# Selections of two sets of heads issued in turn into two PSUM banks, and the places they take in the order of work

## The chip, the cores and the metric

The kernel runs on one core of one Trainium2 chip. The metric is device time in microseconds (us), the median of several runs of the whole program. Engines are named as in the profile: PE (TensorE matmul), PEld (its weight loads), DVE (VectorE), ACT (ScalarE), POOL (GpSimd), SP (SyncE, here only the issuer of DMAs; SPq is its queue).

## The reference

A decoder layer for 32 sequences of 128 tokens with 128 channels, all in float32: causal self-attention with 16 heads of 8 channels, one-head cross-attention to a context, and a mixture of 8 experts (top 2) with a shared expert. Cut to what matters here:

```python
def attn(x, W_attn, b_attn, W_proj, b_proj):          # x (32, 128, 128)
    q, k, v = split(x @ W_attn.T + b_attn)            # 16 heads of 8 channels
    f = cos(ang) + sin(ang)                           # (T, 8)
    att = einsum('bhqd,bhkd->bhqk', q * f, k * f) / sqrt(8)
    att = softmax(where(causal, att, min))
    y = einsum('bhqk,bhkd->bhqd', att, v)
    return y @ W_proj.T + b_proj
x = x + attn(layernorm(x), ...)
x = x + cross_attn(ctx, ctx, layernorm(x), ...)
x = x + moe(layernorm(x), ...)       # probs = softmax(x @ router_w.T), top 2 of 8
```

## The kernel before, in words

The attention stage is a software pipeline over the 32 batches b (sequences). Time is cut into slots s = -4, -3, ...; each entry of the list ORDER is (stage, ahead, part, which), and in slot s every engine goes through the list from top to bottom and does its own share of stage `name` for batch b = s + ahead, if `which` is None or b % 4 == which. So the one list is the program order of PE, ACT, DVE, POOL and SP at once, and each engine is strictly in order. Engines wait for one another by semaphores only.

Batches are projected in groups of four. Two kinds of slot hold selections. A **P slot** (s % 4 == 2) projects the next group (turn_x, project, halves) and selects its first two batches (`("select", 2, j, 0)`). An **R slot** (s % 4 == 3) selects the other two (`("select", 3, j, 2)`), and from slot 11 on it also holds `route`, the choice of experts for an earlier group. P slots are -2, 2, ..., 26; R slots are -1, 3, ..., 27. The steady pattern of four slots repeats; slot s begins at the scores of batch s with part 0.

**select(b, j)**: q and k of a group lie transposed in `qk_hi` and `qk_lo` (a high and a low part), 128 rows by 512 tokens; rows 32j to 32j+31 are the four heads of set j. A selection picks these 32 rows, for two batches, into 96 rows of a PSUM bank: four matmuls (k = 0, 1 for q and k; hi and lo accumulated), 32 rows in, 96 out, 256 columns each. The sets j = 0, 1, 2, 3 use different row groups of the PE array and the four shared banks 1, 3, 2, 0 (`BANK["select"]`). ACT then copies the bank to `qk_stack` (L898), 96 x 512. SP's stack_lo(b) copies from `qk_stack` to `k_slots` and `q_slots` by DMA, once all four sets are there.

**The shared banks.** Every use of one of the four banks is a numbered fill, in the order of the list (`bank_fills`). `w.bank_free(item)` makes PE wait until the reader of the bank's last content has signalled (`drained`); `w.bank_filled(item)` makes the reader wait for PE. Who lies in which bank around the selections:

- bank 0: turn_x2, select 3, values, tall_sums. `values` (PE, L678, 32 records) is probabilities times v.
- bank 1: turn_y, turn_ffn, router, project_v, select 0.
- bank 2: attn_out, xproject, turn_x, project, ranks, select 2.
- bank 3: turn_max, xscores, turn_xprobs, xout, select 1. `xscores` is read by ACT's Exp (L945) after DVE's maximum (L1172); `xout` is read by DVE (L1182).

**Other work near the selections.** `scores(b, j)`: PE L652 and L653 into ps_scores, read by DVE's row maximum L1128. `scores_t(b, j)`: PE L668, read by ACT's Exp L911, then masked on POOL (L551). `route(g)`: DVE L1209 to L1234 in a row; ACT's part is one Exp (L964), for which DVE waits ahead of L1229. `rstd_xattn` is ACT L926 and L928. `attn_out` is PE L697, for which PE waits until ACT has copied the transposed y (L922). `tall_sums` (PE L686, read by DVE L1134) and `turn_y` (PE L692, which waits for DVE's yn, L1137) end a batch's self-attention. `turn_ffn` is PE L734.

In a P slot the places of the selections were, among others: ..., scores 3, scores_t 0, **select 3**, xout, **select 2**, **select 0**, scores_t 1, tall_sums, **select 1**. In an R slot: ..., xscores, scatter, attn_out, **select 0**, norm_ffn, **select 3**, **select 1**, route, rstd_xattn, scores 2, project_v, norm_xattn, **select 2**, values, ... (norm_ffn has no PE work).

After the stage follow the scatter of rows to the experts, the experts' tiles, the shared expert and the output; each hangs on the end of the stage before it.

## Time and profile before

| | |
|---|---|
| median of 3 runs | 520.73 us (518.72 to 522.56) |
| the profiled execution's own time | 523.42 us |
| its span, first to last instruction | 521.7 us |
| mean granted PE clock over the span | 0.945 of full speed |
| granted PE clock between 60 and 300 us | 1.00 |
| instructions | 12081 |

Busy time is the union of an engine's instructions. Matmuls are pipelined, so the records of PE overlap, and what one matmul adds to the chain is less than its own duration. Where the profile gives an idle time of an engine, the engine and line behind the arrow are those that ended it. "issue" is idle time that nothing in the profile explains.

### The profile page before, as it was taken

Reading aid. Unit: us, or ns where it says so; the run is one execution under the profiler, and the core shown is the slowest. Engines: PE = TensorE matmul, PEld = TensorE weight load, DVE = VectorE, ACT = ScalarE, POOL = GpSimd, SP = SyncE. Lnnn points to the kernel's source line nnn. Section 1 sums busy time; section 2 is a strip of 40 time slices with the busy share of each in tenths; the row PEclk is TensorE's granted clock in tenths of the full one; section 3 lists DMA queues with packets and bytes.
Section 4 is the critical chain, followed back from the end, with each engine's and each line's share of the span. In section 5 each row is a group of like instructions: output and inputs, shape, how many; then the busy total and the mean of one; then the engine's idle time right before and its main releaser. Section 6 shows DMA issues by size and latency. Waiting matters only on the chain.

```text
span 521.7 us, 12081 instructions
## 1 busy us (share of the span) xinstructions
PE 447.5 (86%) x3494; PEld 348.2 (67%) x3494; DVE 387.7 (74%) x1262; ACT 320.9 (62%) x975; POOL 282.5 (54%) x369
## 2 busy tenths in 40 slices
PE   1566999999999999999899978459799999898993
PEld 1344667777677677677677756348588877787783
DVE  4473677788988988979889886878467766566585
ACT  1133778888778779788887867542355544454530
POOL 6604263362584775756755666446156655555581
PEclk9967999999999999999999999568899999999997
DMA  6612222221222222222222312512133322222194
GB/s 184 159 38 55 53 57 59 52 64 48 68 70 65 73 72 58 77 66 65 77 59 72 83 41 92 156 37 85 47 83 90 84 81 82 71 76 81 53 355 122
DMA packets 66998, 43.13 MB, mean 83 GB/s; under 512 B 9211, under 2 KB 63878, under 8 KB 66934
## 3 DMA queue, kind: packets, MB, share of 16 engines
q1 hardware_dynamic: 61876, 33.04, 23.6%
q0 software_dynamic: 4320, 8.99, 5.3%
q8 instruction: 30, 0.49, 0.4%
q10 hardware_dynamic: 738, 0.33, 0.2%
q14 instruction: 34, 0.28, 0.2%
HBM read 17.39 MB, written 12.09 MB: 57 GB/s over the span
## 4 chain that ended last, share of the span: by engine, by line
PE 43%; DVE 24%; DMA 11%; issue 8%; SPq 5%; ACT 4%; POOL 3%; DVEq 0%; ACTq 0%; POOLq 0%
PE ps_scores L809 6%; DMA ys<-ctx_t,late 5%; DVE negmax L1128 5%; DMA late<-xs 4%; PE ps_shared L634 3%; PE ps_shared L826 3%; PE ps_shared L678 3%; PE ps_scores L652 3%; PE ps_scores_t L668 3%; PE ps_scores L653 3%; PE ps_shared L622 3%; SPq L415 2%; DMA k_slots<-qk_stack 2%; PE ps_shared L817 2%; PE ps_shared L686 2%
## 5 line engine op out<-in xcount | busy, mean ns | idle before, releaser
L551 POOL TENSOR_SCALAR_AFFINE_SELECT probs<-probs 128x512 f32<-128x512 f32 x128 | 79.9, 635 | 93.6 <-ACT probs L911 92.4
L1128 DVE TENSOR_REDUCE negmax<-ps_scores 128x4 f32<-128x512 f32 x128 | 86.4, 683 | 24.7 <-PE ps_scores L653 24.4
L574 POOL DMA_INDIRECT ys<-ctx_t,late x71 | 68.4, 963 | 61.2 <-ACT ctx_t L1009 58.7
L911 ACT ACTIVATE probs<-ps_scores_t 128x512 f32<-128x512 f32 x128 | 74.4, 596 | 10.4 <-PE ps_scores_t L668 9.5
L544 POOL DMA_INDIRECT xs<-xrow,posu x64 | 65.1, 1017 | 24.8 <-DVE rsum L1250 13.5
L653 PE MATMUL ps_scores<-k_slots,qk_stack 96*128 96x512 f32 x128 | 78.0, 612 | 0.0
L809 PE MATMUL ps_scores<-wide,qk_stack 128*128 x213 | 69.5, 436 | 0.0
L668 PE MATMUL ps_scores_t<-wide,qk_stack 97*128 97x512 f32 x128 | 58.6, 464 | 1.1 <-issue 1.1
L652 PE MATMUL ps_scores<-causal,ident 128*128 128x512 bf16 x128 | 51.1, 399 | 7.8 <-DMA k_slots<-qk_stack 7.6
L1334 DVE COPY probs<-ps_shared 128x256 f32<-128x256 f32 x71 | 30.2, 425 | 25.3 <-PE ps_shared L817 25.3
L999 ACT ACTIVATE qk_stack<-ps_scores_t 128x128 fp32r<-128x128 f32 x71 | 19.7, 278 | 45.9 <-PE ps_scores_t L801 45.9
L826 PE MATMUL ps_shared<-wd,probs 128*128 x284 | 44.2, 279 | 0.1
L1004 ACT ACTIVATE vst<-ps_scores 128x256 f32<-128x256 f32 x71 | 27.3, 384 | 21.3 <-PE ps_scores L809 21.3
L898 ACT ACTIVATE qk_stack<-ps_shared 96x512 fp32r<-96x512 f32 x64 | 35.1, 591 | 8.0 <-PE ps_shared L634 7.5
L809 PEld LDWEIGHTS ps_scores<-wide,qk_stack 128*128 128x128 f32 x213 | 36.2, 195 | 3.2 <-issue 0.2
L826 PEld LDWEIGHTS ps_shared<-wd,probs 128*128 128x128 f32 x284 | 37.8, 193 | 0.4 <-issue 0.3
L678 PE MATMUL ps_shared<-probs,vst 128*32 128x128 f32 x1024 | 35.4, 280 | 0.2 <-POOL probs L551 0.2
L1328 DVE SCALAR_TENSOR_TENSOR vst<-vst,late,ps_scores 128x256 f32<-128x256 f32 x71 | 33.5, 472 | 1.2 <-ACT vst L1004 1.2
L1323 DVE TENSOR_TENSOR qk_stack<-ps_scores_t,qk_stack 128x128 fp32r<-128x128 f32 x71 | 20.7, 292 | 17.1 <-ACT qk_stack L999 13.8
L678 PEld LDWEIGHTS ps_shared<-probs,vst 128*32 128x32 f32 x1024 | 26.6, 111 | 8.2 <-issue 6.9
L668 PEld LDWEIGHTS ps_scores_t<-wide,qk_stack 97*128 97x128 f32 x128 | 25.2, 197 | 8.5 <-issue 3.3
L634 PE MATMUL ps_shared<-qk_hi,picks 32*96 32x256 f32 x128 | 26.8, 322 | 4.2 <-DVE qk_lo L1116 2.4
(229 smaller groups left out, 1163.9 us busy)
## 6 DMA issues: line engine op xcount, KB each, us to landing
k_slots<-qk_stack SPq DMA_DIRECT2D x128, 48.0 KB
wide<-qk_stack SPq DMA_DIRECT2D x128, 48.0 KB
late<-xs SPq DMA_DIRECT2D x71, 66.0 KB
wide<-ys SPq DMA_DIRECT2D x8, 512.0 KB, 7.4
ctx_t<-in_ctx SPq DMA_DIRECT2D x32, 64.0 KB, 2.0
out_x<-res SPq DMA_DIRECT2D x8, 256.0 KB, 3.4
ys<-ctx_t,late POOLq DMA_INDIRECT x71, 2.2
wd<-in_L_ffn_w_down SPq DMA_DIRECT2D x8, 128.0 KB, 3.5
```

The source lines that it names most:

```text
L544: pool.indirect_dma_start(out=xs, out_offset=bass.IndirectOffsetOnAxis(ap=posu[:, g % 2, k, u:u + 1], axis=0), in_=xrow[:, g % 2, k, u, :] ...
L551: pool.affine_select(out=part, in_=part, compare_op=ALU.is_ge, fill=0.0, base=0, pattern=[[0, HJ], [1, T]], channel_multiplier=-1).then_in ...
L574: pool.indirect_dma_start(out=ys, out_offset=bass.IndirectOffsetOnAxis(ap=xload_i[:, i % XL, C + 1:C + 2], axis=0), in_=ybuf[:, i % 4, :], ...
L634: mm = pe.matmul(part, picks[r, k, n].rearrange("p i a d -> p (i a d)"), m[r, k, cs], start=(n == 0), stop=(n == 1))
L652: pe.matmul(PS[j % 2][:], ident16[:], causal[:].rearrange("p a t -> p (a t)"), start=True, stop=False)
L653: pe.matmul(PS[j % 2][:], qk_stack[0:KR, b % RING, j, :], k_slots[:, b % 2, j].rearrange("p a t -> p (a t)"), start=False, stop=True)\
L668: pe.matmul(PT[j % 2][:], qk_stack[0:KR + 1, b % RING, NJ + j, :], q_slots[:, b % 4, j].rearrange("p a t -> p (a t)"), start=True, stop=Tr ...
L678: mm = pe.matmul(bank[VW * i:VW * (i + 1), j * T:(j + 1) * T], vst[:, b % 4, h, :], probs[:, b % 2, h, :], start=True, stop=True, skip_gro ...
L809: mm = pe.matmul(PS[i % 2][:], a[:, i % 4, :], m[:, bass.ds(e, 1), :].rearrange("p a f -> p (a f)"), start=(r == 0), stop=(r == 2))
L826: mm = pe.matmul(PM[i % 2][:, 0:C], xhT[:, i % 3, f * 128:(f + 1) * 128], wd[:, bass.ds(e, 1), f, :].rearrange("p a c -> p (a c)"), start= ...
L911: act.activation(probs[:, b % 2, j * HJ:(j + 1) * HJ, :].rearrange("p a t -> p (a t)"), PT[j % 2][:], ACT.Exp)\
L1128: dve.reduce_max(negmax[:, b % 2, j * HJ:(j + 1) * HJ], PS[j % 2][:].rearrange("p (i t) -> p i t", i=HJ), axis=AX.X, negate=True).then_inc ...
```

## The change

The selections of two sets of heads form a pair. At the place of set 0 in the list PE now issues set 0 and set 1, at the place of set 3 set 3 and set 2: it waits for both banks, and then issues the four matmuls of each in turn, one of the one, one of the other. At the places of sets 1 and 2 PE does nothing. The list is changed so that sets 1 and 2 stand right behind their partners; this moves ACT's copies as well, and the numbering of the bank fills. Nothing is computed otherwise.

```diff
 ORDER = [ ...
     ("halves", 2, 0, 0),
     ("norm_x_stats", 4, None, 0),
     ("select", 3, 0, 2),
+    ("select", 3, 1, 2),
     ("project_v", 1, None, 1),
     ("norm_ffn", -6, None, None),
     ("select", 3, 3, 2),
+    ("select", 3, 2, 2),
     ("norm_x", 3, None, 0),
-    ("select", 3, 1, 2),
     ("route", -11, None, 0),
     ("rstd_xattn", -3, None, None),
     ("scores", 0, 2, None),
...
     ("project_v", 1, None, 0),
-    ("select", 3, 2, 2),
     ("values", -2, None, None),
...
     ("select", 2, 3, 0),          # unchanged
     ("xout", -5, None, None),
     ("select", 2, 2, 0),
     ("select", 2, 0, 0),
+    ("select", 2, 1, 0),
     ("scores_t", -1, 1, None),
     ("tall_sums", -2, None, None),
     ("ranks", -11, None, 0),
-    ("select", 2, 1, 0),
 ]

             def select(b, j):
-                bank = w.bank_free(("select", b, j))
+                if j in (1, 2):
+                    return
+                pair = (j, (1, 0, 0, 2)[j])
+                banks = [w.bank_free(("select", b, i)) for i in pair]
                 w.ge(qk_split, 2 * (b // GB + 1))
-                if b == 0 and j == 0:
+                if b == 0:
                     pe.wait_ge(picked, 1)
-                r, cs = slice(32 * j, 32 * (j + 1)), slice(b % GB * T, (b % GB + 2) * T)
+                cs = slice(b % GB * T, (b % GB + 2) * T)
                 for k in range(2):
-                    part = bank[0:KR, k * 2 * T:(k + 1) * 2 * T]
                     for n, m in enumerate((qk_hi, qk_lo)):
-                        mm = pe.matmul(part, picks[r, k, n]..., m[r, k, cs], start=(n == 0), stop=(n == 1))
-                mm.then_inc(put_bank(("select", b, j)), 1)
+                        for i, bank in zip(pair, banks):
+                            r = slice(32 * i, 32 * (i + 1))
+                            mm = pe.matmul(bank[0:KR, k * 2 * T:(k + 1) * 2 * T], picks[r, k, n]..., m[r, k, cs],
+                                           start=(n == 0), stop=(n == 1))
+                            if k == 1 and n == 1:
+                                mm.then_inc(put_bank(("select", b, i)), 1)
```

## Rows read from the trace of the kernel before

**Rows 1.** From the page's first part: engine, busy us (share of the span), instructions.

```profile
PE 447.5 (86%) x3494; PEld 348.2 (67%) x3494; DVE 387.7 (74%) x1262; ACT 320.9 (62%) x975; POOL 282.5 (54%) x369
```

**Rows 2.** Window, four steady slots: us, busy of PE, PEld, DVE, ACT, POOL; clock; DMA.

```profile
161.30:197.32 36.02, 34.20 (x319) 25.59 (x319) 31.67 (x116) 29.74 (x92) 23.32 (x32) 1.00 0.26 69
```

**Rows 3.** Chain of waits, 182 to 206 us: start us, us, what.

```profile
193.73 0.64 PE ps_shared L634 x4
...
194.78 0.65 PE ps_shared L634 x8
...
196.30 0.64 PE ps_shared L634 x4
...
198.85 0.48 DVE negmax L1128
```

**Rows 4.** Windows within an R slot.

```profile
195.45:200.28 4.83, 4.83 (x32) 3.46 (x32) 3.12 (x9) 4.79 (x14) 2.44 (x4) 1.00 0.13 33
198.90:215.20 16.30, 15.41 (x152) 11.43 (x150) 15.43 (x70) 13.54 (x43) 9.65 (x15) 1.00 0.26 70
```

**Rows 5.** Timeline of PE: start us, us, what [idle before <-releaser].

```profile
215.48 0.30 PE L692 MATMUL ps_shared<-ident,yn 128*128 128x128 f32 x1 [0.56 <-DVE yn L1137]
```

**Rows 6.** Timeline of a P slot.

```profile
194.71 0.37 PE L634 MATMUL ps_shared<-qk_hi,picks 32*96 32x256 f32 x2
...
195.07 0.34 DVE L1182 SCALAR_TENSOR_TENSOR res<-ps_shared,xinv,late 128x128 f32<-128x128 f32 x1
...
195.45 1.08 ACT L898 ACTIVATE qk_stack<-ps_shared 96x512 fp32r<-96x512 f32 x2 [0.45 <-PE ps_shared L634]
...
196.42 0.59 ACT L911 ACTIVATE probs<-ps_scores_t 128x512 f32<-128x512 f32 x1
...
196.98 0.59 ACT L898 ACTIVATE qk_stack<-ps_shared 96x512 fp32r<-96x512 f32 x1
```

**Rows 7.** Timeline of the start-up.

```profile
26.66 0.51 PE L634 MATMUL ps_shared<-qk_hi,picks 32*96 32x256 f32 x4 [2.39 <-DVE qk_lo L1116]
...
27.36 2.05 ACT L898 ACTIVATE qk_stack<-ps_shared 96x512 fp32r<-96x512 f32 x4 [1.65 <-PE ps_shared L634]
```

**Rows 8.** Timeline of an R slot with a route.

```profile
198.78 0.27 ACT L922 ACTIVATE ynT<-ps_shared 128x128 f32<-128x128 f32 x1
...
199.20 0.46 PE L697 MATMUL ps_shared<-wpT,ynT 128*128 128x128 f32 x2
...
200.09 0.19 ACT L945 ACTIVATION_READ_ACCUMULATOR xprobs<-ps_shared,xneg 128x1 f32 x1
200.32 1.56 ACT L898 ACTIVATE qk_stack<-ps_shared 96x512 fp32r<-96x512 f32 x3
200.33 0.15 PEld L634 LDWEIGHTS ps_shared<-qk_hi,picks 32*96 32x96 f32 x1 [0.26 <-ACT xprobs L945]
...
200.87 0.55 DVE L1213 TENSOR_TENSOR sel<-iota,ix 128x32 f32<-128x32 f32 x2
...
201.77 0.23 ACT L964 ACTIVATE mx<-mx 128x36 f32<-128x36 f32 x1
...
202.76 0.16 DVE L1229 TENSOR_SCALAR cwg<-mx 128x4 f32<-128x4 f32 x1
```

**Rows 9.** Timelines of ACT, then DVE, in the first R slot with a route.

```profile
128.29 1.56 ACT L898 ACTIVATE qk_stack<-ps_shared 96x512 fp32r<-96x512 f32 x3
129.74 0.23 ACT L964 ACTIVATE mx<-mx 128x36 f32<-128x36 f32 x1
...
130.44 0.16 DVE L1229 TENSOR_SCALAR cwg<-mx 128x4 f32<-128x4 f32 x1
```

**Rows 10.** Timeline of an R slot without a route.

```profile
93.75 1.57 ACT L898 ACTIVATE qk_stack<-ps_shared 96x512 fp32r<-96x512 f32 x3
...
95.80 1.08 PE L678 MATMUL ps_shared<-probs,vst 128*32 128x128 f32 x32
```

**Rows 11.** Chain of waits behind the last selections.

```profile
274.51 1.01 PE ps_shared L678 x32
```

More of the change, by code:

```diff
@@ L625, in select @@
             def select(b, j):
-                bank = w.bank_free(("select", b, j))
+                if j in (1, 2):
+                    return
+                pair = (j, (1, 0, 0, 2)[j])
+                banks = [w.bank_free(("select", b, i)) for i in pair]
                 w.ge(qk_split, 2 * (b // GB + 1))
-                if b == 0 and j == 0:
+                if b == 0:
                     pe.wait_ge(picked, 1)
-                r, cs = slice(32 * j, 32 * (j + 1)), slice(b % GB * T, (b % GB + 2) * T)
+                cs = slice(b % GB * T, (b % GB + 2) * T)
                 for k in range(2):
-                    part = bank[0:KR, k * 2 * T:(k + 1) * 2 * T]
                     for n, m in enumerate((qk_hi, qk_lo)):
-                        mm = pe.matmul(part, picks[r, k, n].rearrange("p i a d -> p (i a d)"), m[r, k, cs], start=(n == 0), stop=(n == 1))
-                mm.then_inc(put_bank(("select", b, j)), 1)
+                        for i, bank in zip(pair, banks):
+                            r = slice(32 * i, 32 * (i + 1))
+                            mm = pe.matmul(bank[0:KR, k * 2 * T:(k + 1) * 2 * T], picks[r, k, n].rearrange("p i a d -> p (i a d)"), m[r, k, cs],
+                                           start=(n == 0), stop=(n == 1))
+                            if k == 1 and n == 1:
+                                mm.then_inc(put_bank(("select", b, i)), 1)
             def project_v(b):
```

## The prediction

> **What bounds the kernel now.** I began with the page's busy lines: TensorE (PE) is busy for 86% of the span, VectorE (DVE) for 74% [rows 1]. That mixes stages, so next I took the windows of the attention stage, the only one that the edit touches. There, 36.02 us, one group of four slots, hold 34.20 us of PE, 31.67 of DVE and 29.74 of ScalarE (ACT) [rows 2]. None can be dismissed, and the question is who waits for whom at the selections. The chain of waits answers it. Through a P slot the chain lies on PE: the selections stand in it as three pieces, 0.64, 0.65 and 0.64 us, and PE hands over to DVE at 198.85 [rows 3]. From there the chain is DVE alone until 215.3: in 198.90 to 215.20 DVE is busy for 15.43 of 16.30 us [rows 4]. At its end PE is the one that waits, 0.56 us for DVE's yn [rows 5]. So in an R slot PE has time to give, and DVE has none.
>
> The reader is to see one more thing in these rows: the piece of 0.65 us is "x8". Two selections that stand next to each other in program order already run side by side: their first matmuls appear as one record "x2" of 0.37 us at 194.71 [rows 6], and eight matmuls take what four take alone (0.65 against 0.64). In the start-up, where no bank is waited for, four selections ran together: four first matmuls in 0.51 us, and ACT's first evacuation 0.70 us after the first of them started [rows 7]. Selections of different row groups and banks overlap when they are adjacent and no wait stands between them. Turn-by-turn issue adds nothing to that; what counts is which selections become adjacent, and what they wait for.
>
> **The change part by part.** It adds and removes no operation. It removes two places per group: in a P slot three runs of selections (3; 2 and 0; 1) become two, in an R slot three (0 and 3; 1; 2) become one run of two pairs. In PE time that is 0.64 us in a P slot and 2 x 0.64 = 1.28 us in an R slot. Each pair now waits for both of its banks before its first matmul.
>
> P slot, pair 3 and 2: bank 2's last content (xproject) is gone when PE gets there, so this costs nothing, and select 2 moves 1 us earlier, into the 0.45 us in which ACT sat idle before its evacuation at 195.45 [rows 6].
>
> P slot, pair 0 and 1: bank 3 holds xout, issued just before it. It is read by DVE's L1182, 195.07 to 195.41 [rows 6], and DVE gets to it no sooner. In the kernel before, select 2 and 0 started at 194.71 without it. A woken PE starts about 0.05 us after its releaser (L634's load at 200.33 after the record of L945 that ends at 200.28) [rows 8], so the pair starts at 195.46, 0.75 us later. The run that stood alone at 196.30, 0.64 us [rows 3], is gone, and with it some 0.1 us of refilling ahead of the transpose at 196.94. Later by 0.75, shorter by about 0.75: the P slot comes out even. I take 0, with bounds of -0.2 and +0.7 (no refilling saved and the wait fully added).
>
> ACT behind it: before, it was busy from 195.45 to 200.28 with 4.79 of 4.83 us [rows 4]. Evacuations in a row take 0.49 us each after the first (three in 1.56 us, at 0.59 for the last) [rows 8]. After: two evacuations from 195.46 + 0.74 = 196.20, where 0.74 is the distance from the pair's start to its evacuation in the rows (194.71 to 195.45) [rows 6], then the Exp that stood between (196.42 to 196.98, 0.56). It is through at 197.73, where it was through at 196.98 + 0.49 = 197.47 [rows 6]. ACT enters the R slot 0.26 us late and, having no idle time, carries this to L945. The transposed y on ACT (L922, ends 199.05) is late by the same; PE's attn_out (L697, 199.20) had 0.12 us to spare and is late by 0.14 us [rows 8].
>
> R slot: the first pair needs bank 3, where xscores lies until ACT's L945 has read it. This wait is in the trace already, ahead of select 1 alone: PE's load at 200.33 waited for L945, which ended at 200.28 [rows 8]. Select 0 and 3 had gone ahead of it, so that ACT could go from L945 straight to three evacuations at 200.32 [rows 8]. After, all four selections wait: start at 200.33 + 0.26 = 200.59, ACT idle until 200.59 + 0.74 = 201.33. Four evacuations, select 2's with them, take 4 x 0.485 = 1.94 us. ACT's Exp of the route (L964, 0.23 us) stands behind all of them in ACT's order: it starts at 203.27 and ends at 203.50, against 201.77 before [rows 8].
>
> Who waits for that: DVE's L1229. It started at 202.76 [rows 8] and had 0.76 us of slack. With the 0.14 us from above it would arrive at 202.90; it now starts at 203.55. The DVE chain grows by 0.79, say 0.80 us, in a slot in which DVE sets the end, and behind L1229 are queued the row maxima of scores and all of the DVE chain to 215.3. The same distances stand in the slots of 161, 197 and 233 us, three in all. In the first slot with a route DVE was quicker (L1229 at 130.44, L964 at 129.74, evacuations from 128.29 [rows 9]): 128.30 + 0.26 + 0.74 + 1.94 + 0.23 + 0.05 = 131.52, so 1.05 us there, rounded down by the little slack behind it.
>
> R slots whose end PE sets: values uses bank 0, in which select 3 lies. In the R slot of 90.74 the evacuations began at 93.75 and values started at 95.80 [rows 10]. After: ACT is 0.1 us late there, so 93.85 + 0.74, then two evacuations at 0.49 and 0.59 for the third, and 0.05: 96.20, or +0.40 us. In the last one (slot 27) the chain goes through values (274.51) to the loads of k_slots [rows 11]; the same sum with 0.26 in place of 0.1 gives +0.57. Before these, the start is bound by DMA issue and by ACT, whose number of evacuations is unchanged: 0. Nothing is selected after 27, and what follows hangs on the end of this stage one for one.
>
> Sum: 0.40 + 1.05 + 3 x 0.80 + 0.57 = +4.4 us. The profiled execution took 523.42 us around a span of 521.7; it would take 527.8. It lay 2.7 us above the median of the three runs, 520.73, so I name 520.73 + 4.4 = 525.1 us, +0.8%. A measurement of this kernel can tell about 1% (5.2 us) from nothing.
>
> The trace shows the two selections in one record x2 of 0.37 us, though all four matmuls of the first stand ahead of the second's in program order [rows 6]. The Trainium skill, "TensorE: Matmul & The Clock Gate", Part 3, says that matmuls start in strict program order and that only weight loads are pulled ahead. That would make the alternation necessary for any overlap; the trace does not agree, and what it would give is rival E below. Eight matmuls take 0.65 us, but each of the two banks takes ACT 0.49 us [rows 3, 8], and that is what my sum rests on. The Trainium skill, "TensorEngine Tiling (Array Packing)", PSUM Bottleneck, warns of just this: tiling speeds up TensorE, not the copies out of PSUM.
>
> **The rivals.** (B) Faster: PE's time is the bound after all, and ACT's lateness finds cover. For it: 34.20 of 36.02 us of PE [rows 2], the chain on PE in P slots and in the first and last R slots. Against: PE's wait of 0.56 us behind DVE [rows 5]. It saves 0.64 + 1.28 us per group, less 0.66 us of waiting for L1182 beyond xout's end, 1.26; over the six groups with xout 7.6 us: 513.1. It decides if the route's Exp still ends before DVE asks, that is if ACT's four evacuations start no later than 200.7 (202.9 less 1.94 and 0.23).
>
> (A) Lateness absorbed: the route's Exp is late but DVE gets its time back from less contention (its two sel operations at L1213 took 0.55 us beside GpSimd [rows 8]). Then only the slots where PE sets the end count, 0.40 + 0.57: 521.7.
>
> (C) Slower still: the P slot does not come out even, since the alone-standing select 1 filled time that PE now spends waiting for scores' readers. Six times 0.66 us on top of the sum, 4.0: 529.1. For it: the chain of a P slot is PE throughout [rows 3]. It decides if the transposes behind scores_t start later than they did.
>
> (D) It does not do what it says: issued in turn, the two row groups hinder each other and a pair costs two selections, 1.28 us. Three pairs of each group then add 0.63 us to the path (both in a P slot, the first in an R slot), over six groups 11.3: 536.4. Against it: x2 and x4 in one record [rows 6, 7].
>
> (E) Overlap comes only from alternation. Against it is the piece of 0.65 us for eight matmuls [rows 3]; for it nothing in this trace. It would take one selection's 0.64 us off each of the two pairs in a P slot, six groups: 7.7 us off the sum, 517.4. It is the result that the strict order of the Trainium skill (the section named above) would give.
>
> **How the numbers follow.** Forecast (+2.5 to +6.5 us) 0.54, A 0.14, B 0.13, C 0.13, D 0.05, E 0.01. The forecast's own range is 523 to 527.5. For 8 in 10 the range goes down into B and up past C: 516 to 530.5; left out are most of B and D. Faster by over 1% (under 515.5): 0.13, from B. Slower by over 1% (over 525.9): C, D and four tenths of the forecast, 0.40. Within 1%: the rest, 0.47, which holds A and the larger part of the forecast.
>
> **What would show it.** In the changed kernel's trace: in R slots PE idle 0.7 us before L634 with ACT L945 as its releaser, four evacuations in a row, L964 about 1.5 us later against L945 than before, and DVE waiting for ACT L964 ahead of L1229 for 0.6 to 1.0 us. In P slots: PE waiting for DVE L1182, 0.6 us, and the next slot's first maximum no earlier than before. The steady four slots take 36.8 instead of 36.0 us. I am wrong if L1229 starts without a wait, if sixteen matmuls take clearly more or less than 0.7 us, or if the four slots shrink.

## The result and the profile after

The changed kernel took 530.31 us (median of 4, 529.57 to 531.11) against 520.53 for the kernel before (518.72 to 522.56) on the same chip: ratio 1.0166, 95% interval 1.0117 to 1.0215, by which it is some 8.6 us slower (the two medians lie 9.8 us apart). The forecast was +4.4 us, in the right direction and about half of it. The profiled execution took 529.62 us around a span of 527.8, 6.1 us longer than the span before.

From the page of the changed kernel, the busy line that answers to [rows 1] and two groups of instructions (behind the bar: idle time ahead of them and its releaser). Lines behind select are 7 higher than before: L639 is the selection (L634 before), L905 ACT's evacuation of a bank, its copy to `qk_stack` (L898), L685 values (L678), L952 xprobs' Exp (L945), L971 the route's Exp (L964), L1236 cwg (L1229), L1189 the reader of xout (L1182).

```profile
PE 441.9 (84%) x3494; PEld 342.5 (65%) x3494; DVE 386.7 (73%) x1262; ACT 320.6 (61%) x975; POOL 282.3 (53%) x369
...
L905 ACT ACTIVATE qk_stack<-ps_shared 96x512 fp32r<-96x512 f32 x64 | 33.5, 591 | 14.7 <-PE ps_shared L639 14.5
...
L685 PE MATMUL ps_shared<-probs,vst 128*32 128x128 f32 x1024 | 36.3, 285 | 3.5 <-ACT qk_stack L905 3.3
```

The same two groups in the kernel before:

```profile
L898 ACT ACTIVATE qk_stack<-ps_shared 96x512 fp32r<-96x512 f32 x64 | 35.1, 591 | 8.0 <-PE ps_shared L634 7.5
...
L678 PE MATMUL ps_shared<-probs,vst 128*32 128x128 f32 x1024 | 35.4, 280 | 0.2 <-POOL probs L551 0.2
```

PE's share fell from 86 to 84%, and the two costs are in the idle columns: ACT now waits 14.5 us for selections (7.5 before), and values waits 3.3 us for ACT, which it did not before. How much of this is path shows in the windows. From the first scores of slot 8 to those of slot 28 (five groups of four slots), before and after:

```profile
99.52:278.30 178.78, 170.61 (x1588) 128.11 (x1587) 156.99 (x575) 148.76 (x457) 108.68 (x148) 1.00 0.25 66
```

```profile
101.20:286.31 185.11, 168.33 (x1588) 124.94 (x1587) 156.13 (x574) 148.95 (x457) 108.85 (x148) 0.97 0.24 64
```

The stretch grew by 6.33 us, which is all of the span's growth; outside it, losses in the start-up and gains after slot 28 cancel. The column to see is PEclk: 1.00 before, 0.97 after. By slot, 10, 11, 14, 15, 19 and 22 in turn (10, 14, 22 are P slots, the others R):

```profile
116.23:127.01 10.78, 9.82 (x90) 7.03 (x90) 8.46 (x25) 8.68 (x25) 2.60 (x5) 1.00 0.25 65
127.01:136.34 9.33, 8.21 (x90) 6.11 (x89) 7.71 (x36) 8.14 (x26) 2.85 (x5) 1.00 0.16 41
152.72:164.20 11.48, 10.55 (x90) 7.60 (x90) 8.72 (x26) 9.37 (x26) 5.90 (x9) 0.94 0.27 75
164.20:174.34 10.14, 8.80 (x89) 6.53 (x89) 7.68 (x35) 7.91 (x25) 4.75 (x7) 0.90 0.20 54
201.64:212.53 10.89, 9.78 (x90) 7.39 (x89) 8.46 (x38) 8.22 (x26) 4.86 (x7) 0.84 0.22 58
228.10:239.83 11.73, 10.79 (x90) 7.74 (x90) 8.72 (x26) 9.43 (x26) 6.15 (x9) 0.91 0.27 73
```

Two kinds of slot stand here. At full clock a P slot takes 10.78 us (10.73 before) and an R slot 9.33 (8.91 before). In slots 14 and 15, 19, and 22 (and 23, not shown) the clock is below full and they take up to 1.6 us more. Slots 14 to 16 lost 1.68 us that way against undisturbed ones, 19 and 20 together 0.80 (19 lost 1.57, 20 gave back 0.77), 22 and 23 1.48: 3.96. The rest, 5 x 0.41 in R and on average 5 x 0.07 in P slots, is 2.4 us. Together 6.36.

The mechanism inside a P and the following R slot (timeline of the changed kernel, start and duration in us; it answers to [rows 6] and [rows 8]):

```profile
199.34 0.34 DVE L1189 SCALAR_TENSOR_TENSOR res<-ps_shared,xinv,late 128x128 f32<-128x128 f32 x1
...
199.83 0.36 PE L639 MATMUL ps_shared<-qk_hi,picks 32*96 32x256 f32 x2 [0.76 <-DVE res L1189]
...
200.55 1.08 ACT L905 ACTIVATE qk_stack<-ps_shared 96x512 fp32r<-96x512 f32 x2 [0.79 <-PE ps_shared L639]
...
203.66 0.46 PE L704 MATMUL ps_shared<-wpT,ynT 128*128 128x128 f32 x2
...
204.50 0.19 ACT L952 ACTIVATION_READ_ACCUMULATOR xprobs<-ps_shared,xneg 128x1 f32 x1
...
204.75 0.48 PE L639 MATMUL ps_shared<-qk_hi,picks 32*96 32x256 f32 x4 [0.63 <-ACT xprobs L952]
...
205.49 2.05 ACT L905 ACTIVATE qk_stack<-ps_shared 96x512 fp32r<-96x512 f32 x4 [0.79 <-PE ps_shared L639]
...
205.52 0.39 PE L659 MATMUL ps_scores<-causal,ident 128*128 128x512 bf16 x1
...
207.11 1.94 PE L685 MATMUL ps_shared<-probs,vst 128*32 128x128 f32 x32 [0.48 <-ACT qk_stack L905]
...
207.42 0.24 ACT L971 ACTIVATE mx<-mx 128x36 f32<-128x36 f32 x1
...
207.69 0.17 DVE L1236 TENSOR_SCALAR cwg<-mx 128x4 f32<-128x4 f32 x1 [0.37 <-ACT mx L971]
```

In the P slot PE idles 0.76 us until DVE has read xout (L1189). In the R slot all four selections wait 0.63 us for L952's read-out, then run four abreast: "x4" of 0.48 us, and the next matmul behind all sixteen starts at 205.52, 0.77 us after the first. Four evacuations follow, the route's Exp L971 starts at 207.42, and DVE's L1236 waits for it. That is the predicted chain of events. What was not predicted is the row of values, 32 matmuls in 1.94 us. The same row in slot 27, where the clock is full:

```profile
282.46 1.08 PE L685 MATMUL ps_shared<-probs,vst 128*32 128x128 f32 x32 [0.48 <-ACT qk_stack L905]
```

And the granted clock around the values of slot 19 (first three windows) and in slot 14 (the last two), in the changed kernel:

```profile
206.00:207.00 1.00, 0.63 (x3) 0.30 (x2) 0.86 (x6) 1.00 (x4) 0.87 (x1) 1.00 0.34 90
207.20:210.40 3.20, 3.20 (x40) 2.72 (x41) 1.89 (x11) 1.83 (x8) 0.00 (x0) 0.50 0.33 84
210.70:212.50 1.80, 1.80 (x16) 1.47 (x15) 1.67 (x8) 1.32 (x5) 0.50 (x1) 1.00 0.23 64
```

```profile
162.80:166.10 3.30, 3.30 (x14) 2.36 (x12) 1.24 (x3) 2.50 (x7) 1.27 (x2) 0.50 0.08 20
166.20:174.34 8.14, 6.80 (x83) 5.19 (x82) 6.90 (x33) 6.71 (x22) 3.63 (x5) 1.00 0.25 67
```

A clock of 0.50 is the lower of TensorE's two levels, 1.2 GHz. In slot 19 the fall comes at the end of PE's waits of 0.63 us (for L952) and 0.48 us (for L905); in slot 14 it comes at 162.7, behind the wait of 0.76 us for L1189, though the other P slots have the same wait, and slots 10, 18 and 26 had no fall behind it. So the open questions were: is the clock what cost 4 us, is it PE's new waits that lower it, and which of them; and why did an R slot lose 0.41 and not 0.80.

### The profile page after: what moved, and what is told of

It reads as the page before. It is cut to its first block, busy times and chain, and to the rows that moved or that the text cites. A ratio compares the mean times of both kernels' runs of the same rounds, so it can differ in the third digit from the quotient of the medians.

```text
span 527.8 us, 12097 instructions
## 1 busy us (share of the span) xinstructions
PE 441.9 (84%) x3494; PEld 342.5 (65%) x3494; DVE 386.7 (73%) x1262; ACT 320.6 (61%) x975; POOL 282.3 (53%) x369
## 4 chain that ended last, share of the span: by engine, by line
PE 31%; DVE 26%; DMA 8%; issue 7%; ACT 5%; SPq 3%; POOL 1%; DVEq 0%; ACTq 0%; POOLq 0%
DVE negmax L1135 7%; PE ps_scores L816 6%; DMA ys<-ctx_t,late 4%; PE ps_shared L833 3%; DMA late<-xs 3%; PE ps_scores_t L675 2%; ACT qk_stack L905 2%; PE ps_shared L824 2%; PE ps_scores L770 2%; PE ps_shared L784 2%; PE ps_shared L639 2%; DVE xn L1166 2%; PE ps_scores_t L770 2%; SPq L415 1%; PE ps_scores_t L808 1%
## 5 line engine op out<-in xcount | busy, mean ns | idle before, releaser
L551 POOL TENSOR_SCALAR_AFFINE_SELECT probs<-probs 128x512 f32<-128x512 f32 x128 | 80.0, 638 | 101.5 <-ACT probs L918 100.5
L660 PE MATMUL ps_scores<-k_slots,qk_stack 96*128 96x512 f32 x128 | 79.3, 622 | 0.0
L675 PE MATMUL ps_scores_t<-wide,qk_stack 97*128 97x512 f32 x128 | 60.3, 477 | 1.2 <-issue 1.0
L905 ACT ACTIVATE qk_stack<-ps_shared 96x512 fp32r<-96x512 f32 x64 | 33.5, 591 | 14.7 <-PE ps_shared L639 14.5
L685 PE MATMUL ps_shared<-probs,vst 128*32 128x128 f32 x1024 | 36.3, 285 | 3.5 <-ACT qk_stack L905 3.3
L685 PEld LDWEIGHTS ps_shared<-probs,vst 128*32 128x32 f32 x1024 | 27.2, 113 | 11.9 <-issue 6.2
L659 PEld LDWEIGHTS ps_scores<-causal,ident 128*128 128x128 bf16 x128 | 15.5, 121 | 21.3 <-issue 17.7
```

What stands on the lines that cost most here:

```text
L551: pool.affine_select(out=part, in_=part, compare_op=ALU.is_ge, fill=0.0, base=0, pattern=[[0, HJ], [1, T]], channel_multiplier=-1).then_in ...
L659: pe.matmul(PS[j % 2][:], ident16[:], causal[:].rearrange("p a t -> p (a t)"), start=True, stop=False)
L660: pe.matmul(PS[j % 2][:], qk_stack[0:KR, b % RING, j, :], k_slots[:, b % 2, j].rearrange("p a t -> p (a t)"), start=False, stop=True)\
L675: pe.matmul(PT[j % 2][:], qk_stack[0:KR + 1, b % RING, NJ + j, :], q_slots[:, b % 4, j].rearrange("p a t -> p (a t)"), start=True, stop=Tr ...
L685: mm = pe.matmul(bank[VW * i:VW * (i + 1), j * T:(j + 1) * T], vst[:, b % 4, h, :], probs[:, b % 2, h, :], start=True, stop=True, skip_gro ...
L905: act.activation(qk_stack[0:KR, s:s + 2, j::NJ, :].rearrange("p u k t -> p k u t"), bank[0:KR, :].rearrange("p (k u t) -> p k u t", k=2, u ...
```

## The experiments

The stretch from slot 8 to slot 28 is given for each kernel, since it holds all that the edits touch in the steady state. What lies outside it (span less stretch) ranged from 339 to 348 us over the profiles: 339.3 to 342.9 in the six whose R slots have no common wait of all four selections for bank 3 (before, before_again, e1, e2, e3, e8), 342.7 to 347.8 in the eight that issue both pairs there. Of that difference only 0.4 us is located, in slot 7 (9.1 to 9.2 us long against 8.7 to 8.9). Much else varies there: slot 0 began 3.7 us later in after_again and e11 than in the rest, and e6 lost 3.6 us shortly before its end. So a single profile's span is no measure of an edit, and the pairs of R slots may cost something outside the stretch as well. A "fall" is a stretch at 1.2 GHz within these slots. "Group" is the length of four slots at full clock, from the starts of slots. The ratio is that of timed executions to those of the kernel before on the same chip. That kernel's own median was 523.84 us beside e1 to e4, 522.72 beside after_again, e5, e6 and e9, and 523.21 beside e8, e10 and e11, where the expectations count from 520.5: read them 2 to 3 us higher.

| kernel | ratio, 95% interval | slots 8 to 28, us | falls | group, us |
|---|---|---|---|---|
| before | 1 | 178.78 | 0 | 36.02 |
| before_again | - | 180.39 | 1 (slot 10) | 36.02 |
| after | 1.0166 (1.0117 to 1.0215) | 185.11 | 3 (14, 19, 22) | 36.5 |
| after_again | 1.0154 (1.0102 to 1.0206) | 187.13 | 4 (10, 14, 18, 26) | 36.46 |
| e1_order_only | 1.0019 (0.998 to 1.0058) | 179.30 | 1 (26) | 35.79 |
| e2_turns_only | 0.9993 (0.9953 to 1.0032) | 180.39 | 1 (26) | 36.02 |
| e3_p_only | 1.0063 (1.0026 to 1.0099) | 183.39 | 3 (10, 14, 26) | 36.17 |
| e4_r_only | 1.0091 (1.0057 to 1.0124) | 180.37 | 0 | 36.32 |
| e5_route_first | 1.0111 (1.0072 to 1.0150) | 181.05 | 1 (10) | 35.81 |
| e6_filled | 1.0118 (1.0062 to 1.0175) | 180.84 | 0 | 36.42 |
| e9_p_filled | 1.0071 (1.0032 to 1.0109) | 180.79 | 0 | 36.40 |
| e11_route_filled | 1.0057 (1.0018 to 1.0095) | 183.75 | 3 (11, 23, 27) | 35.83 |
| e8_p_late | 1.0022 (0.9989 to 1.0056) | 179.65 | 0 | 36.20 |
| e10_late_route | 1.0031 (0.999 to 1.0071) | 179.42 | 0 | 35.82 |

**e1_order_only: the new order, the old select.** In the changed kernel, select(b, j) is the function of before, set by set, each with its own wait.

> The new order of the selections, but each of the four sets issued by itself with its own wait, as before the change. My theory is that the change loses time through the waits that a pair takes together: in R slots nothing may start until ACT's xprobs Exp (L952) has been read out, in P slots the pair 0 and 1 waits for DVE's reader of xout (L1189), and on top of it TensorE's granted clock fell after these idle stretches in three places. With its own wait, select 0 goes ahead in both slots and only select 1 waits. ACT then has one evacuation to do at once and three behind it: the route's Exp comes about 0.5 us earlier than in the changed kernel, and DVE's L1236 waits 0 to 0.2 us instead of 0.4 to 0.6. PE's new idle time is about half. I expect 521 to 524 us, so at least 6 us faster than the changed kernel. Rival 1, the order itself costs the time (select 1 and 2 stand too early, whoever waits): 528 to 531 us. Rival 2, the turns cost it: as the kernel before, 520 to 521 us, with the clock at full in every slot.

It took 1.0019 times the kernel before, 524.97 us, and 1.4% less than the changed kernel; rival 1 is out. Timeline of its R slot 19:

```profile
199.99 0.35 PE L634 MATMUL ps_shared<-qk_hi,picks 32*96 32x256 f32 x1
...
200.49 0.19 ACT L945 ACTIVATION_READ_ACCUMULATOR xprobs<-ps_shared,xneg 128x1 f32 x1
...
200.73 0.38 PE L634 MATMUL ps_shared<-qk_hi,picks 32*96 32x256 f32 x3
200.74 2.30 ACT L898 ACTIVATE qk_stack<-ps_shared 96x512 fp32r<-96x512 f32 x4
...
202.92 0.24 ACT L964 ACTIVATE mx<-mx 128x36 f32<-128x36 f32 x1
...
203.19 0.17 DVE L1229 TENSOR_SCALAR cwg<-mx 128x4 f32<-128x4 f32 x1
```

Select 0 goes first, so ACT has an evacuation at hand when L945 is through and has work again 0.06 us later; the other three selections start together ("x3") at 200.73, beside that evacuation. DVE's L1229 starts at 203.19 without a wait, 2.70 us behind L945's read-out; in the changed kernel it is 3.19. A group is even 0.23 us shorter than before. So neither the order nor the overlap costs time; the common wait does. One fall (slot 26) hides the gain in this profile: that group took 37.50 us.

**e2_turns_only: turns alone.** The order of before; the two places with two neighbours are issued in turn, with the changed kernel's loop over both banks.

```diff
-                bank = w.bank_free(("select", b, j))
+                partner = {(0, 2): (0, 0), (2, 0): (2, 3)}   # (b % 4, set) -> its neighbour
+                if (b % GB, j) in partner.values():
+                    return
+                pair = (j,) if (b % GB, j) not in partner else (j, partner[b % GB, j][1])
+                banks = [w.bank_free(("select", b, i)) for i in pair]
...
```

> The order of the kernel before, with the two places at which two selections already stood next to each other (2 and 0 in a P slot, 0 and 3 in an R slot) issued matmul by matmul in turn, waiting for both banks first. Neither of these banks is what the other waits for. My theory says that turns change nothing, since neighbours overlapped before: 520 to 522 us, the eight matmuls in 0.65 us as before. Rival D of the prediction, turns hinder: each such place costs another 0.3 to 0.6 us, 525 to 532 us. Rival E, overlap is better in turns: below 518 us.

0.9993 (523.0 us): no difference, and the groups are 36.02 us to 0.01. Rivals D and E of the prediction are both out. The one fall (slot 26) is the whole 1.6 us of the stretch's surplus.

**e3_p_only and e4_r_only: half of the change each.** The same code with other pairs: `{(0, 3): (0, 2), (0, 0): (0, 1), (2, 0): (2, 3)}` with the new P order, and `{(0, 2): (0, 0), (2, 0): (2, 1), (2, 3): (2, 2)}` with the new R order.

> P slots as in the changed kernel (3 and 2, then 0 and 1, in turns, waiting for DVE's reader of xout), R slots as in the kernel before with 0 and 3 in turns. By the waits the undisturbed P slot is even (10.79 against 10.73 us), so six times 0.06, under 1 us. If the granted clock falls here too (PE idles 0.76 us ahead of the pair), up to 1.3 us for each time: I expect 521 to 523 us with no or one such place. Rival C of the prediction, the P slot is what costs: 526 to 530 us. A third view, that the idle stretch in P slots is what lowers the clock: two to three places with the clock below full, 524 to 526 us.

> R slots as in the changed kernel (all four sets behind the wait for L952, in pairs), P slots as in the kernel before with 2 and 0 in turns. By the waits an R slot grows by 0.41 us in the five slots from 11 on and 0.4 in slot 7: 2 to 2.5 us. With the clock falling as in the changed kernel, up to 4 us more. I expect 523 to 527 us, and DVE waiting 0.3 to 0.5 us for ACT ahead of L1236. Rival C (the P slot costs, R does not): 520 to 522 us. If both slots' waits are needed together for the clock to fall, the clock is at full here and the time is 522.5 to 523.5 us.

```profile
100.24:283.63 183.39, 171.56 (x1588) 128.70 (x1587) 156.14 (x575) 149.16 (x457) 108.53 (x148) 0.97 0.24 65
```

```profile
100.34:280.71 180.37, 167.27 (x1588) 123.67 (x1587) 156.22 (x574) 148.60 (x457) 108.65 (x148) 1.00 0.25 66
```

The halves add up: 0.63 + 0.91 = 1.54%, against 1.66 and 1.54 for the whole. They cost in different ways. e3 (first row) has the P slot's wait (0.76 us), groups only 0.15 us longer at full clock, and three falls. e4 (second row) has groups 0.30 us longer and no fall; DVE's wait ahead of L1236 is there (0.41 us in slot 19). The expectation that clock falls are few in e3 was wrong, the third view written there (the P slot's idle stretch lowers the clock) fits. e4's timed surplus (0.91%, 4.7 us) is more than its profile shows (1.6 us, and 0.3 in slot 7). This one profile is no fair sample of its clock either: over its twelve timed executions the granted clock was lower than in the kernel before (figures below, with the falls counted).

**after_again: the changed kernel once more.**

> The changed kernel unaltered, to see what is fixed in it and what varies. My theory: the lengths of its slots at full clock repeat to 0.05 us (P 10.79, R 9.32), while the places where TensorE's granted clock falls are different ones, two to four of them, each 0.8 to 1.7 us. I expect 527 to 531 us. Rival: the three places of the first profile (slots 15, 19 and 23) come back exactly, then something in those slots, not the idle stretch common to all of them, lowers the clock. Second rival: no fall of the clock in this execution and the time still near 530, then the clock does not explain the missing 4 us.

```profile
103.78:290.91 187.13, 169.60 (x1562) 125.23 (x1587) 156.15 (x574) 149.41 (x456) 108.51 (x148) 0.96 0.24 64
```

The undisturbed lengths repeat, the falls do not: slots 10, 14, 18 and 26, all of them P slots, four instead of three. With 5 x 0.48 us for the waits taken off, four falls cost 187.13 - 178.78 - 2.4 = 5.95, 1.5 us each. The ratio repeats, 1.0154. (Some PE records are missing from this trace, and from those of e5, e6 and e9: PE's counts and busy time are too low there.)

**e6_filled and e9_p_filled: PE kept busy in its waits.** In the changed kernel, ahead of the wait for the second bank; e9 has also `and b % GB == 0`, that is P slots only.

```diff
-                banks = [w.bank_free(("select", b, i)) for i in pair]
+                banks = [w.bank_free(("select", b, pair[0]))]
+                if j == 0 and b >= GB:
+                    ...
+                    w.ge(qk_split, 2 * (b // GB + 1))
+                    for _ in range(6):      # select 0's first matmul, into its own bank
+                        pe.matmul(banks[0][0:KR, 0:2 * T], picks[r0, 0, 0]..., qk_hi[r0, 0, c0], start=True, stop=True)
+                banks.append(w.bank_free(("select", b, pair[1])))
```

> The changed kernel with six more matmuls, issued ahead of the pair that holds selection 0, in P and R slots: copies of selection 0's first matmul into its own bank, which selection 0 then overwrites, run after that bank is free and before the wait for bank 3. They fill the 0.63 to 0.76 us in which PE idled. They add work and take no wait away, so by waits alone the kernel can only be as slow or slower: 529 to 532 us (rival 1). My theory says that what they fill is what made the granted clock fall: full clock in all attention slots, slots as in the changed kernel at full clock (P 10.8 to 10.9, R 9.3 to 9.4), and 3 to 4 us back: 525 to 528 us. Rival 2: the clock falls because of the amount of work in some longer stretch, or by chance: two or three places with the clock below full, as in the changed kernel, 529 to 532 us.

> As the kernel with six more matmuls, but these only in P slots, ahead of the pair 0 and 1. With P slots alone changed the clock fell in two places, with R slots alone changed in none. If the idle stretch of 0.76 us ahead of the pair in a P slot is what matters, filling it alone gives the clock back as filling both does: 525 to 528 us, no place below full. If the stretch of the R slot (0.63 us) is as harmful, one to three places remain: 527 to 530 us.

The P slot of e9 (timeline; L635 are the six matmuls, L645 the selections, L1195 the reader of xout, L911 the evacuation), and its stretch:

```profile
161.62 0.94 PE L635 MATMUL ps_shared<-qk_hi,picks 32*96 32x256 f32 x6
161.98 0.34 DVE L1195 SCALAR_TENSOR_TENSOR res<-ps_shared,xinv,late 128x128 f32<-128x128 f32 x1
...
162.37 0.35 PE L645 MATMUL ps_shared<-qk_hi,picks 32*96 32x256 f32 x2
...
163.12 1.08 ACT L911 ACTIVATE qk_stack<-ps_shared 96x512 fp32r<-96x512 f32 x2 [0.74 <-PE ps_shared L645]
```

```profile
102.06:282.85 180.79, 167.82 (x1591) 124.85 (x1617) 156.35 (x574) 147.75 (x456) 108.64 (x148) 1.00 0.24 66
```

Six matmuls that compute nothing new stand in the hole, 0.75 us of it, and the pair starts 0.05 us after DVE's reader, as before. No wait is shorter, and the clock is full in all twenty slots of both. e9's stretch is 4.3 us shorter than in the changed kernel and 6.3 shorter than in its second profile. e9 is also faster in timed runs: 1.0071 (1.0032 to 1.0109) against 1.0166 and 1.0154. For e6 the timed runs don't show it: 1.0118, with an interval (up to 1.0175) that holds the changed kernel's ratio, from six executions. Its median of 530.06 us lies above the 525 to 528 us expected, even if these are read 2 us higher. What lay outside its stretch took 348 us in the profile, the longest of all.

**e5_route_first: the route ahead of the second pair.**

```diff
     ("select", 3, 1, 2),
+    ("route", -11, None, 0),
     ("project_v", 1, None, 1),
...
     ("norm_x", 3, None, 0),
-    ("route", -11, None, 0),
```

> The changed kernel with the route of the group moved ahead of the second pair of selections in the order (between selections 0, 1 and selections 3, 2 of an R slot), on every engine. ACT's route Exp (L971) then stands behind two evacuations instead of four, 0.97 us earlier. My theory says that DVE's wait at L1236 (0.37 us) goes and an R slot of the changed kernel (9.32) comes back to about 8.95, five times 0.4 less: 2 us off the changed kernel's time by this term. The falls of the clock come from PE's waits, which stay (P 0.76 us, R 0.63 us): so 526 to 529 us, with PE losing the clock in one to three places. Rival 1: the R slot is late for the wait of PE itself (0.63 us) and not for the route: R stays at 9.3, 529 to 531 us. Rival 2: the delayed evacuations 3 and 2 now hold up values and scores: R above 9.4.

```profile
204.96 0.48 PE L639 MATMUL ps_shared<-qk_hi,picks 32*96 32x256 f32 x4 [0.62 <-ACT xprobs L952]
...
205.70 1.08 ACT L905 ACTIVATE qk_stack<-ps_shared 96x512 fp32r<-96x512 f32 x2 [0.79 <-PE ps_shared L639]
...
206.67 0.23 ACT L971 ACTIVATE mx<-mx 128x36 f32<-128x36 f32 x1
...
206.79 1.07 ACT L905 ACTIVATE qk_stack<-ps_shared 96x512 fp32r<-96x512 f32 x2
...
207.28 0.15 DVE L1236 TENSOR_SCALAR cwg<-mx 128x4 f32<-128x4 f32 x1
```

L971 starts 1.71 us after the first selection, in the changed kernel 2.67: the 0.96 expected. L1236 starts without a wait. The expected 0.4 us did not show where I had put it, the R slot is 9.44 long; the next slot is 6.97 instead of 7.73, and the group is 35.81 instead of 36.4 to 36.5, 0.6 shorter. So it is by the route's lateness behind the evacuations that the R slot costs. Four evacuations ahead of it are harmless if they start early: e1 has them too, but the first starts 0.25 us behind L945's read-out and not 0.99, and nothing is lost. The gain of 0.6 us is more than the 0.41 lost, so a part of it may be the earlier place's own; no run moves the route in the kernel before. The timed ratio, 1.0111, gained less than that, and its interval overlaps the changed kernel's.

**e11_route_filled: both mends.** The order of e5 with the matmuls of e9.

> The two mends together on the changed kernel: the route ahead of the second pair in R slots, and six extra matmuls in P slots ahead of the pair 0 and 1 (copies of selection 0's first matmul, overwritten by it). At full clock four slots with the route moved took 35.82 us, against 36.5 in the changed kernel and 36.02 in the kernel before. If the extra matmuls keep the clock as they did before, all four steady groups take 35.8 to 35.9 us and the time is 521.5 to 524 us, no worse than the kernel before by more than 0.3%. Rival 1: the two terms are not independent, the clock falls again at one to two places through PE's wait in R slots: 524 to 527 us. Rival 2: moving the route costs something outside the steady groups (slots 0 to 7 or 28 on): 524 to 527 us with full clock.

```profile
243.26 0.48 PE L645 MATMUL ps_shared<-qk_hi,picks 32*96 32x256 f32 x4 [0.63 <-ACT xprobs L958]
...
245.74 1.93 PE L691 MATMUL ps_shared<-probs,vst 128*32 128x128 f32 x32 [0.60 <-ACT qk_stack L911]
```

```profile
104.69:288.44 183.75, 171.11 (x1617) 129.00 (x1617) 156.34 (x576) 148.34 (x457) 108.63 (x148) 0.97 0.24 65
```

1.0057, the best of the kernels in which a pair waits for xout's reader, but rival 1 is what the profile shows: groups of 35.83 us, no fall in a P slot, and three in R slots. In each of them the clock falls at values, behind waits of 0.63 and 0.60 us, as it did in slot 19 of the changed kernel (0.63 and 0.48). This profile is of its longest execution, 532.13 us where the other eleven took 521.6 to 529.2, so its falls are not to be taken for the usual number.

**e8_p_late and e10_late_route: no wait for xout's reader in the P slot.** Both have the pair 0 and 1 at the old place of select 1; e8 with the R slots of before, e10 with those of e5.

```diff
     ("select", 2, 3, 0),
+    ("select", 2, 2, 0),
     ("xout", -5, None, None),
-    ("select", 2, 2, 0),
-    ("select", 2, 0, 0),
     ("scores_t", -1, 1, None),
     ("tall_sums", -2, None, None),
     ("ranks", -11, None, 0),
+    ("select", 2, 0, 0),
     ("select", 2, 1, 0),
```

> P slots: the pair 3 and 2 early, the pair 0 and 1 together at the place where selection 1 stood alone (behind scores_t, tall_sums and ranks), so that two runs of selections remain, and neither waits: bank 3's xout has long been read there. R slots as in the kernel before, 0 and 3 in turns. My theory: without PE's wait no fall of the clock in the steady groups, and a P slot shorter by up to one run of selections, 0.2 to 0.6 us: steady groups 35.4 to 35.8 us, 518 to 521 us. Rival 1: selection 0's evacuation now falls into the time in which ACT is full, and pushes xprobs (L952) later by 0.5 us, which delays PE and ACT in the R slot: P shorter, R longer, 36.0 to 36.4 us for four slots, 521 to 524 us. Rival 2: DVE is the bound in P slots too: nothing changes, 520.5 to 522 us.

> The P slots of the kernel with the late pair 0 and 1 (no wait for DVE's reader of xout), and the R slots of the kernel with the route ahead of the second pair. If both work as each by itself, steady groups 35.2 to 35.7 us, no fall of the clock (R slots alone showed none), 517 to 521 us. Rival: both changes load ACT ahead of the route's Exp, so that the R slot is as late as in the changed kernel (9.3 us and a next slot of 7.73): 522 to 525 us.

```profile
197.15 0.36 PE L639 MATMUL ps_shared<-qk_hi,picks 32*96 32x256 f32 x2
...
197.89 1.08 ACT L905 ACTIVATE qk_stack<-ps_shared 96x512 fp32r<-96x512 f32 x2 [0.41 <-PE ps_shared L639]
...
198.54 0.33 PE L741 MATMUL ps_shared<-ident,xrow 128*128 128x128 f32 x1 [0.68 <-ACT qk_stack L905]
```

No fall in either, and the gain expected of e8 is not there: 0.18 us per group lost. PE's turn_ffn (L741), which comes next in its bank, waits 0.68 us for ACT's evacuation of select 0. The wait had only moved. e10 has e5's short groups (35.82) and no fall in slots 8 to 28, and still no gain over the kernel before (1.0031). So 1.0022 and 1.0031 are the best of the kernels with both pairs in a P slot, and none of the versions beats the kernel before.

**before_again: a second profile of the kernel before.**

> The kernel before unaltered, a second profile, to see whether it loses the clock too. Two kernels with nearly its order lost it once each, in the last P slot (26). I expect none or one fall in slots 8 to 28, and slots at full clock that repeat to 0.05 us (P 10.73, R 8.91); 178.8 to 180.5 us from slot 8 to slot 28, against 185.1 and 187.1 in the two profiles of the changed kernel. If two or more falls show here, the clock is no part of the difference.

Its slots are the same to 0.04 us, and slot 10 with 11 took 1.60 us more, with a fall. So the kernel before loses its clock too, but seldom.

**The falls counted.** Over all fourteen profiles, slots 10, 14, 18, 22, 26 and 11, 15, 19, 23, 27:

| slot and what PE does there | falls |
|---|---|
| P, waits 0.76 to 0.9 us for xout's reader (after, after_again, e3, e5) | 10 of 20 |
| P, the same wait filled with matmuls (e6, e9, e11) | 0 of 15 |
| P, waits 0.65 to 0.68 us at the slot's end, for ACT (e8, e10) | 0 of 10 |
| P, no wait over 0.35 us (before, before_again, e1, e2, e4) | 3 of 25 |
| R, all selections wait 0.62 to 0.85 us for L952 (after, after_again, e4, e5, e9, e10, e11) | 4 of 35 |
| R, no such wait, or filled (the other seven) | 0 of 35 |

Three of the four falls in R slots are those of the one profile of e11. The first row holds 2, 4, 3 and 1 falls in its four profiles.

A profile is one execution, but every timed execution has its mean granted clock over the whole program on record. In the kernel before, that mean was 0.958 in each of three sets (84 executions in all, single ones from 0.94 to 0.97; a mean of twelve is good to some 0.003). It was 0.949 and 0.950 in the two sets of the changed kernel (4 and 6), 0.952 in e3, 0.951 in e4, 0.949 in e5, 0.954 in e1 and e9, 0.955 in e10, 0.956 in e8, and 0.958 in e2, e6 and e11. An estimate from the changed kernel's span: 0.009 less of 528 us, at half speed, is some 9.5 us more at 1.2 GHz in every execution, while e6, with both waits filled, has none more than the kernel before. e4, without a fall in its profile's steady slots, lost as much clock as e3 in its twelve executions, so the R slot's wait is not free of this cost. And e6 has its clock back but not its time (1.0118): the clock is not the whole of what the sum missed.

## Why the prediction was half right

- **Turns do nothing, neighbours overlap anyway.** Right: e2. Sixteen matmuls took 0.77 us, predicted "0.7". The Trainium skill, "TensorE: Matmul & The Clock Gate", Part 3 (strict program order), would have asked for turns; the measurement decides against it, for matmuls of different row groups and banks.
- **P slot even.** Right for the waits: the pair starts 8.98 us after the slot's start (190.85 to 199.83; 8.88 forecast), the slot takes 10.78 to 10.79 against 10.73. Rival C, with its price of 0.66 us, did not come by waiting.
- **R slot, the chain of events.** Right, and by e1 and e5 the cause: four evacuations that start late, ahead of the route's Exp. y's projection L704 came 2.02 us after the slot's start, 1.88 before: the 0.14 forecast.
- **R slot, the size.** Mis-sized: +0.80 forecast, +0.41 measured, for two reasons. (The forecast sets the new end of the route's Exp, 203.50, beside 201.77, where it started before; it ended at 202.00. The sum goes by the slack of 0.76 us and isn't touched by this.) First, ACT's lateness of 0.26 shrank to 0.21 at the slot's start and 0.10 at L952 (204.24 - 201.64 = 2.60, before 2.50), so L1236 came 6.05 us after the slot's start against 5.44: +0.61. Second, DVE won 0.2 back in the next slot, in two operations that took 0.11 us less each than before. They stand next to POOL's mask (L551), and start later against it; that this is the reason is not shown (before, then e9, as the changed kernel's slot 20 follows a fall):

```profile
206.97 0.76 DVE L1244 TENSOR_TENSOR sel<-sel,rank 128x32 f32<-128x32 f32 x2
...
208.09 0.44 DVE L1248 CAST posu<-posf 128x8 uint32<-128x8 f32 x1
```

```profile
210.87 0.65 DVE L1257 TENSOR_TENSOR sel<-sel,rank 128x32 f32<-128x32 f32 x2
...
211.88 0.33 DVE L1261 CAST posu<-posf 128x8 uint32<-128x8 f32 x1
```

  That is the effect named in rival A, time won back by DVE, for a quarter of its size; I had it as all or nothing. Slot 11 (+1.05 forecast) and 27 (+0.57) also grew by 0.41, slot 7 by 0.42 (9.20 against 8.78; +0.40 forecast). The waits make 0.42 + 5 x 0.41 + 5 x 0.07 = 2.8 us in place of 4.4.
- **The missing term.** The sum took PE's clock for granted: it was 1.00 in [rows 2] and from 60 to 300 us, and no step asked what an idle stretch in a P slot would do to it. The change adds to PE ten such stretches in the five groups (five of 0.76 to 0.9 and five of 0.63 us, where the waits for xout's reader and for L952 had been covered by other selections). Three and four falls came with them, 1.3 and 1.5 us each on average, 4.0 and 6.0 us. The step that failed is "the P slot comes out even": in waiting, yes; but its price is paid in the clock. e9 shows it by filling the hole: no fall in its profile, and 1.0071 in place of 1.0154 to 1.0166. The Trainium skill, the same page, "A second HAM failure mode: psum-queue depth-cycling", tells of a kernel in which short idling of PE between groups of matmuls made the clock go back and forth; the traces here agree, with idling of 0.76 us.
- **Against "what would show it".** Seen: PE idle before L639 behind L952 (0.63; 0.7 forecast), four evacuations in a row, L971 later against L952 by 1.24 (1.5), DVE's wait 0.37 (0.6 to 1.0: too small). P slots: wait for L1189 0.76 (0.6). Four slots: 36.4 to 36.5 at full clock (36.8), 38.0 with a fall. The median of 530.31 lay outside the forecast's own range (523 to 527.5) and 0.2 us inside the end of the wide one, which reached that far for rival C, a longer P slot. The 4 us that brought it there are in no rival, so that the wide range held it is luck.

**Open.** Why a given wait is followed by a fall and the next one is not; the falls differ between two profiles of one kernel. Why three falls came in P slots without the wait, and why R slots had three in e11 and none in e5 and e10, whose R slots are the same. Why e4, e5 and e6 are slower in timed runs than their profiles' slots would make them by 2 to 4 us: for e4 and e5 the lower clock of their timed executions is a part, and all three have pairs in R slots, with the longer rest of the program that goes with them and is not located.

## What to carry to other kernels

When work that needs different buffers is joined, it waits for the last of them together, and whoever consumes it gets it in one lump: look at what stands behind that lump on the consumer's engine (here the route's Exp behind four evacuations), and keep separate waits where the buffers come free at different times (e1 kept the overlap and lost nothing). When an edit turns a covered wait into idle time of TensorE, even under 1 us and even where the path does not get longer, price the clock too: compare the granted clock slot by slot, and take more than one profile.

## What the runs showed of the hardware

- Selections of four row groups into four banks, in pairs by turn, run four abreast: sixteen matmuls of 256 columns in 0.77 us, against 0.64 for four. In e1 three sets issued one after the other, not in turn, also started as "x3" of 0.38 us.
- TensorE fell to 1.2 GHz in 10 of 20 slots in which it idled for 0.76 to 0.9 us in a busy stretch, and in 0 of 15 with the same hole filled by useless matmuls. Idle stretches of 0.62 to 0.85 us elsewhere were followed by a fall in 4 of 45 slots, and 3 of 25 slots without one had a fall too. A fall cost 0.7 to 1.7 us (slot 14 of e3, slot 26 of e1) of a path of which PE was only part.
- The same kernel had three falls in one profile and four, elsewhere, in the next, while its slots at full clock repeated to 0.05 us.
